# Mixture-of-experts stage: 71 slots of 256 rows become 60 slots of 256 rows and 15 tiles of 128 rows

## The reference

```
h = layernorm(x) * (1 + cb) + sb
logits = h @ router_w.T                      # 8 experts
weights, indices = top_k(softmax(logits), 2) # 2 of 8 for each of 8,192 tokens
weights = weights / (weights.sum(-1) + 1e-6)
gate, up = split(h @ w13[e])                 # 256 -> 2 x 512
y_e = (silu(gate) * up) @ w2[e]              # 512 -> 256
x = x + gb * sum over the two chosen e of weights * y_e
```

## Time and profile before

| | before |
|---|---|
| median of 3 runs | 1293.57 us (1293.27 to 1296.74) |
| time of the profiled execution | 1293.22 us |
| its span | 1291.4 us |
| expert stage, first to last matmul | about 713 to 1276 us |
| PE busy over the span | 1152.0 us, 89% |
| DVE / ACT / POOL busy | 906.8 / 713.2 / 929.5 us |

### The profile page before, as it was taken

The page is one execution under the profiler, slowest core; times in us unless marked ns, Lnnn a source line. Parts: engine busy times, 40 slices in busy tenths (PEclk is TensorE's granted clock), DMA queues, the critical chain, the costliest instruction groups (busy, mean ns, idle before and its releaser), DMA issues. The chain is left out here.

```text
span 1291.4 us, 53384 instructions
## 1 busy us (share of the span) xinstructions
PE 1152.0 (89%) x19576; PEld 978.8 (76%) x19576; DVE 906.8 (70%) x2387; ACT 713.2 (55%) x1419; POOL 929.5 (72%) x990
## 2 busy tenths in 40 slices
PE   4699999999999999999623899999999999999995
PEld 1477778888777777787413788888888888888884
DVE  2589999999999999999888544444444444444442
ACT  2378888988889888898533233333333333333331
POOL 3168999999899999999822466666666667676653
PEclk8599999999899999999655999999999999999998
DMA  8323343334333334333355688878788887888860
GB/s 223 82 69 82 94 138 116 90 106 123 100 104 111 106 108 118 97 118 101 100 155 148 124 137 128 136 136 134 137 135 137 127 131 136 133 139 136 136 108 1
DMA packets 201704, 153.07 MB, mean 119 GB/s; under 512 B 101658, under 2 KB 179570, under 8 KB 201330
## 3 DMA queue, kind: packets, MB, share of 16 engines
q0 software_dynamic: 32592, 56.75, 27.4%
q1 hardware_dynamic: 160770, 81.89, 25.0%
q10 hardware_dynamic: 8096, 11.01, 3.3%
HBM read 63.58 MB, written 44.04 MB: 83 GB/s over the span
## 5 line engine op out<-in xcount | busy, mean ns | idle before, releaser
L1298 PE MATMUL psum<-xT,xall 128*128 128x256 f16 x3408 | 384.8, 273 | 14.9 <-DMA xT<-grow 14.9
L1298 PEld LDWEIGHTS psum<-xT,xall 128*128 x3408 | 334.0, 98 | 54.3 <-issue 15.2
L1360 POOL DMA_INDIRECT out<-late,sidx x142 | 227.0, 1599 | 167.0 <-DVE late L1349 80.1
L1306 ACT ACTIVATE sg<-psum 128x512 f32<-128x512 f32 x142 | 84.8, 597 | 281.6 <-PE psum L1298 281.6
L1311 DVE SCALAR_TENSOR_TENSOR late<-psum,sg 128x512 f32<-128x512 f32 x142 | 98.2, 692 | 185.0 <-ACT sg L1306 182.9
L1278 POOL DMA_INDIRECT grow<-moe_rows,gidx x142 | 146.1, 1029 | 86.9 <-DVE gidx L1150 44.0
L1332 PE MATMUL psum<-w2s,hT 128*128 x1704 | 197.7, 273 | 2.8 <-DVE w2s L1386 2.6
L1332 PEld LDWEIGHTS psum<-w2s,hT 128*128 128x128 f16 x1704 | 166.6, 98 | 22.8 <-issue 3.4
L1322 DVE TENSOR_TENSOR hT<-late,hT 128x512 f16<-128x512 f32 x142 | 98.4, 693 | 98.7 <-ACT hT L1318 98.7
L1318 ACT ACTIVATE hT<-late 128x512 f16<-128x512 f32 x142 | 89.4, 629 | 112.0 <-DVE late L1311 112.0
L672 POOL TENSOR_TENSOR pT<-sc,pT 128x1024 f16<-128x1024 f32 x64 | 136.5, 2134 | 11.7 <-ACT pT L668 11.7
(11 more groups left out here) (262 smaller groups left out, 2294.2 us busy)
## 6 DMA issues: line engine op xcount, KB each, us to landing
stk<-qk SPq DMA_DIRECT2D x384, 64.0 KB, 2.9
moe_rows<-hrows SPq DMA_DIRECT2D x64, 256.0 KB, 3.6
out<-xall SPq DMA_DIRECT2D x64, 128.0 KB, 3.3
raw<-in_w ACTq DMA_DIRECT2D x26, 256.0 KB, 3.3
xall<-in_x ACTq DMA_DIRECT2D x16, 256.0 KB, 4.0
raw<-in_w SPq DMA_DIRECT2D x8, 512.0 KB, 8.9
xall<-in_x SPq DMA_DIRECT2D x8, 384.0 KB, 8.1
grow<-moe_rows,gidx POOLq DMA_INDIRECT x142, 4.7
```

The source lines that it names most:

```text
L1298: i = k.e.matmul(bank[:, n * LONG:(n + 1) * LONG], w13s[:, bass.ds(ex_reg * (G * 4 * I) + ((2 * c + b_) * 2 * I + col), P)], xT[:, k.x, a, ...
L1306: done(k.e.activation(sg[:, half, :], bGate[half][:, :], ACT.Silu, scale=1.0 / W_SCALE), "sg")
L1360: k.e.indirect_dma_start(out_rows, bass.IndirectOffsetOnAxis(ap=sidx[:, n:n + 1], axis=0), yo[:, k.v, q, :], None, bounds_check=B * T - 1, ...
```

## The change

The list has `NSLOT_TILES` = 135 tiles in place of 142: each expert's rows are now rounded up to whole tiles (128 + 7). Whole pairs of an expert's tiles are numbered first, then the odd ones. `NPAIRED` = 60 slots take tiles 0 to 119 in pairs as before; 15 slots, the singles, take the tiles 120 to 134 one by one. The units run in groups of five, `ORDER` = "PPSPP", 15 groups. With the counts given above there are 64 pairs and 3 odd tiles: tiles 120 to 127 are full tiles, 128 to 130 hold 111, 22 and 82 rows, and 131 to 134 hold none.

A pair unit is handled as a slot was. A single goes another way:

- `gate_up_by_token`: 12 matmuls in which the tile's transposed rows stand still and 512 columns of the weights move, into two PSUM banks of its own (6 and 7). The result has tokens on partitions.
- `silu_by_token`, `h_mul_by_token`, `h_hi_by_token`, `h_lo_by_token`: the same four steps, once for the tile, on 128 x 512.
- `h_trans`: two transposing DMAs on SP turn the high and the low part, since `down` needs hidden units on partitions. They are issued behind `x_trans` of the unit three places later.
- `down`: 12 matmuls of 256 columns. `gather`, `x_trans` and `scatter`: one transfer each.

Routing gets more DVE steps: pair and odd counts, three small maps that say where an expert's tiles lie, two steps on the tile numbers, and the expert of each slot in two passes. The router weights' ring `wrow` is `NWR` = 4 deep and its chain uses another semaphore.

```diff
-NSLOTS = (B * T * 2) // LONG + E - 1
-NSLOT_TILES = 2 * NSLOTS
+NSLOT_TILES = (B * T * 2) // P + E - 1
+NPAIRED = ((B * T * 2) // P - E) // 2
+NSLOTS = NSLOT_TILES - NPAIRED
+ORDER = "PPSPP"
...
+    def gate_up_by_token(k):
+        x_here(k)
+        k.product_done(1)
+        ex_reg = k.expert()
+        for c in range(G):
+            for a, b_ in PARTS:
+                for bank, at in ((bGate1, 0), (bUp1, I)):
+                    i = k.e.matmul(bank[:, :], xT[:, k.x, a, c, 0:P],
+                                   w13s[:, bass.ds(ex_reg * (G * 4 * I) + ((2 * c + b_) * 2 * I + at), I)],
...
+    def h_trans(k):
+        if k.n > 0:
+            k.e.wait_ge(S["y"], k.u - len(ORDER) + 1)
+        k.high_done()
+        k.e.dma_start_transpose(hT1[:, 0, :, :], hrow1[:, 0, :]).then_inc(s_hT, 16)
+        k.low_done()
+        k.e.dma_start_transpose(hT1[:, 1, :, :], hrow1[:, 1, :]).then_inc(s_hT, 16)
...
     def scatter(k):
         k.wait("yw")
-        k.wait_added(1)
-        for q in range(2):
-            n = 2 * k.t + q
+        k.moved(s_sc, V, k.u - 1)
+        for q, n in enumerate(k.tiles):
             k.e.indirect_dma_start(out_rows, ...
...
         @block.sync
         def _(e):
             route_sync(e)
-            for t in range(NSLOTS):
-                x_trans(Slot(e, t))
+            for u in range(NUNITS + NXT + 1):
+                k, single = unit(e, u), unit(e, u - NXT - 1)
+                if single and single.single:
+                    h_trans(single)
+                if k:
+                    x_trans(k)
...
+            for group in range(NUNITS // len(ORDER)):
+                gate_up(p0, 0)
+                gate_up(p0, 1)
+                if before:
+                    down(before)
+                gate_up(p1, 0)
+                gate_up(p1, 1)
+                down(p0)
+                gate_up_by_token(single)
+                down(p1)
+                gate_up(p2, 0)
+                gate_up(p2, 1)
+                gate_up(p3, 0)
+                down(single)
+                gate_up(p3, 1)
+                down(p2)
+            down(p3)
```

More of the change, by code:

```diff
@@ L1129, in route_vector @@
             if k == 0:
[L1130 to L1134, removed]
@@ L1150, in route_vector @@
         e.tensor_scalar(gidx[:, :], rowf[:, :], 0.0, None, ALU.max).then_inc(s_idx, 1)
[L1151 to L1154, removed]
+        for x_ in range(0, E - 1):
+            link(e.scalar_tensor_tensor(out=ex_of[:, :], in0=at, scalar=single_end[:, x_:x_ + 1],
                                         in1=ex_of[:, :], op0=ALU.is_ge, op1=ALU.add))
@@ L1267, in done @@
+            return expert_of[self.slot]
+    UNIT_OF_PAIR = [u for u in range(NUNITS) if not Unit(None, u).single]
     def done(ins, stage):
@@ L1337, in row_weights @@
     def row_weights(k):
[L1338 to L1343, removed]
+        k.moved(s_g, U, k.u)
+        late.link(k.e, k.e.tensor_tensor(gwm[:, k.r, 0:k.nq, :], grow[:, k.j, 0:k.nq, 2 * D:ROW],
+                                         bc_mid(oh_tile[:, k.slot, :], k.nq), ALU.mult))
+        k.wait("yw", NWR)
+        late.link(k.e, k.e.tensor_reduce(wrow[:, k.r, 0:k.nq], gwm[:, k.r, 0:k.nq, :], axis=X, op=ALU.add))
     def weigh(k):
         k.wait("y")
[L1346 to L1350, removed]
+        k.moved(s_sc, V, k.u - V)
+        for q in range(k.nq):
+            i = k.e.scalar_tensor_tensor(out=yo[:, k.v, q, :], in0=bY[k.y][:, q * D:(q + 1) * D],
+                                         scalar=wrow[:, k.r, q:q + 1], in1=grow[:, k.j, q, D:2 * D], op0=ALU.mult,
                                          op1=ALU.mult)
@@ L1371, in _ @@
             route_tensor(e)
-            for t in range(NSLOTS + 2):
-                now, late = slot(e, t - 1), slot(e, t - 2)
-                if now:
-                    gate_up(now, 0)
-                if now:
-                    gate_up(now, 1)
-                if late:
-                    down(late)
+            for group in range(NUNITS // len(ORDER)):
+                before, (p0, p1, single, p2, p3) = unit(e, group * len(ORDER) - 1), [unit(e, group * len(ORDER) + i) for i in range(5)]
+                gate_up(p0, 0)
[14 more added lines that the diff above has]
+            down(p3)
         @block.vector
@@ L1407, in _ @@
             route_scalar(e)
-            for t in range(NSLOTS):
-                for half in range(2):
-                    silu(Slot(e, t), half)
-                    h_hi(Slot(e, t), half)
+            for u in range(NUNITS):
+                k = unit(e, u)
+                if k.single:
+                    silu_by_token(k)
+                    h_hi_by_token(k)
+                else:
+                    for half in range(2):
+                        silu(k, half)
+                        h_hi(k, half)
         @block.gpsimd
@@ L1414, in _ @@
             route_gpsimd(e)
-            for t in range(NSLOTS + U - 1):
-                ahead, late = slot(e, t), slot(e, t - U + 1)
+            for u in range(NUNITS + U - 1):
+                ahead, late = unit(e, u), unit(e, u - U + 1)
                 if ahead:
```

253 lines of the change are left out of this document (177 added, 76 removed).

## The result

| | before, measured alongside | after |
|---|---|---|
| median | 1291.52 us (1287.61 to 1299.72, 20 runs) | 1285.53 us (1281.15 to 1294.59, 20 runs) |
| ratio, 95% interval | | 0.9968, 0.9953 to 0.9983 |
| profiled execution: its span | 1291.4 us | 1283.7 us |
| first to last matmul of the expert stage | 562.8 us | 555.6 us |

What follows compares the result with a forecast made beforehand. PE bounds the kernel, with the scatter chain right behind, taking over after the change: 1291.4 - 27.9 + 2.4 + 2.4 = 1268.3, + 15.1 for the chain = 1283.4 us, as a median 1285.5; range 1270 to 1298.

Steps and rivals of the forecast that it cites:

- PE's saving: PE in the expert stage: matmul time falls from 557.7 to 529.8 us, saving 27.9 us; a group takes 35.34.
- Routing: Routing on DVE and ACT: extra steps make `gidx` later and add 2.4 us to the path, bounds 0 and 3.5.
- The tail: Last scatters: the last two units become full pairs, landings cost at least 3.2 us each instead of 2.00, +2.4 us.
- There are 2.2 us to spare: SP's transposes before `down(single)`: ready at 8.3 us, due at 10.48, so free while POOL is less than 2.2 us late.
- The way that it named: With POOL over 2.2 us late, SP is held at a gather and PE waits at `down(single)`, 1 to 2 us a group.
- This is the term that decides: POOL's serial scatter chain: a group needs 36.68 us against PE's 35.34, so it ends 15.1 us behind PE.
- the single's link: Scatter chain: a single's scatter takes 5.80 us, a pair's 7.72 less one issue of 1.92; named as the likeliest error.
- The pair's link: Scatter chain: a pair's scatter stays at 7.65 to 7.80 us, taken as 7.72, from the trace before the change.
- Rival 1: PE stays the bound and the scatter chain keeps up, links averaging under 7.45 us: 1270 us, up to 1275; chance 0.2.
- Rival 2: More transposes lengthen scatter landings, making it slower: 1309 us at full, 1293 to 1298 partly; chance of over 1297.5: 0.12.
- The chip's clock: PE's clock: should not follow if PE waits a few us at `down(single)`, but left open; a fall would show as 0.50.
- the waits' lines: Sign in POOL's waits: nearly all of `out` for the DMA, few for DVE, if the scatter chain sets the pace.

Runs made afterwards that it cites:

- the second profile: The changed kernel, unaltered, measured and profiled once more against the kernel before: 1279.42 us, ratio 0.9923, expert stage 547.4 us.
- the run with both edits: Changed kernel with the single's transposes issued ahead of `x_trans(s+3)` and the expert's number loaded before the waits of `gate_up`: 1265.74 us, ratio 0.9800.
- the first experiment: Changed kernel with the expert's number read into PE's register before the waits of `gate_up` instead of behind them: 1280.57 us, ratio 0.9909.

## Why the number was right and the mechanism wrong

**PE's saving: right.** 27.9 us was worked out, from 35.34 us for a group. Where PE doesn't wait, a group takes just that: in the run with the transposes moved, from the end of one `gate_up_by_token` at 910.46 to the next at 945.80. The matmuls of 512 columns, bounded from the earlier trace rows, take 0.216 us: from 765.11 to the next matmuls at 767.70 it is 2.59 us for 12 (the 2.75 of the line run to the modelled end of the last).

```profile
765.11 2.75 PE L1382 MATMUL psum<-xall,xT 128*128 x12
```

**Routing: right.** +2.4 us was forecast. From the first step of routing on DVE to the last step of `gidx` it was 29.80 us and is 32.12, +2.3; the first matmul starts 1.9 us later behind the same point. The attention half before it, which the change leaves alone, ended 2.9 us sooner in this execution (between 661 and 669 us in the profiles), so 2.9 of the 7.7 us between the two spans are not the change's.

**The tail: mis-sized.** +2.4 was forecast, +0.5 measured. The last landing is waited for 2.97 us in place of 2.00, near the 3.2 taken; but it is the only one that counts, since the scatter before it waits for DVE (2.72 us) and not for a landing.

**"There are 2.2 us to spare": the step that failed first.** Two of its numbers were short. The rows of s+3 were there later than +1.2: at +3.9 in the timeline above, whose last gather started at -0.7 (-3.2 to -2.6 at 11 other singles), and the transposes left the queue at +6.8 to +9.2, not +6.3. And the transposes landed not 2 us behind their issue but, at the eight stalls in the two profiles of the changed kernel, 3.6 to 6.6 us. The prediction had its bound at a gather's 4.7 and took 2, between the ends, without a row for it. With 4.5 in place of 2 the spare is -0.3 us even if POOL is on time. There is a slip in the sum too: a gather issued at -2.5 lands by its 4.7 us at +2.2, not +1.2, which alone takes 1.0 of the 2.2 us. The way that it named, SP held at a gather and PE waiting at `down(single)`, is what happened; but its condition, POOL more than 2.2 us late, was not needed. It held at the single of the timeline, whose gather was 2.5 us late; at the other stalls of that profile, and at all ten of the run without the singles' scatters, POOL was on time.

**"This is the term that decides": the step that fell.** The scatter chain was to end 15.1 us behind PE. Three things speak against it: with 15 links fewer the stage stayed at 555.6 us; with all links kept but the transposes issued first it fell to 538.7; and in that run the chain's links average 35.0 us a group, just under PE's 35.34. The size that was wrong is above all the single's link: 5.80 was taken, the pair's less one issue, and it is 5.0 in the mean there and 4.8 in the middle. With 5.0 and the pair's 7.72 left as it was, a group is 35.88 us and the lag 0.5 us, not 1.34; with the pair's 7.5 there is none. The prediction had named this itself as where it would be wrong above all. The pair's link was taken from a stretch of the trace of before whose pace need not be the chain's floor; its last link ends at a wait for DVE. That a term of 15.1 us was wrong and the time right is chance: PE stood still by another way. Its idle time in the stage, over the matmuls worked out, was 562.8 - 557.7 = 5.1 us before and 555.6 - 529.8 = 25.8 after, 20.7 us more, nearly all at the two places named. So the stage has -27.9 + 20.7 = -7.2 us; with routing's +1.9, the tail's +0.5 and the -2.9 of the attention half that makes the -7.7 us of the spans. And 14.2 of the 20.7 us are of a sort that the second profile doesn't have (last section), so even this way to 1285.5 us belongs in part to one execution.

**The rivals.** Rival 1, "PE stays the bound", 1270 us, was wrong for the kernel as changed and right in that the chain doesn't bind: with the transposes moved ahead that is the time, 1269.34 us. Rival 2, landings of the scatters lengthened by more transposes, is not seen: in the run with the transposes moved, which has all 30 of them, a pair's link averages 7.5 us, under the 7.65 to 7.80 of before. But the transposes themselves land late. The rule of the Trainium skill ("DMA: Bandwidth & Descriptors", "Queues, rings and completion order"), that a semaphore increment lands only behind the earlier writes of its DMA engine, would make a transpose's landing wait for scatters and gathers in flight; 3.6 to 6.6 us agree with that, but no run here takes away the transfers that are in flight at that time, so it is not shown.

**The chip's clock.** Left open was whether it would fall when PE waits a few us. It did not: 1.00 over the stretch in which PE stands still 17 us.

## What to carry to other kernels

Give a transfer its place on an in-order queue by when its data are ready, and never behind an instruction that waits for a later unit's data: moving two issues one unit forward took the ratio from 0.9968 (0.9923 in the second measurement) to 0.9828, more than the whole change had gained. A stall taken away in front of one that binds later only moves (1.2 us less before `gate_up(p3)`, 1.3 more before `down(single)`, both stages 538.7 us), so look at the length of the stage and not at the stall's line; and a spare of 2 us that rests on a landing nobody has measured is no spare. When a forecast time comes out, still look whether its releasers are those forecast: here the waits' lines gave the first doubt. They are no proof: the run with the transposes moved has 26 waits for landings, 60.5 us in all, that cost PE nothing. What decides is to take the suspected work away and read the stage.

## What the hardware showed that was not expected

**Landings of small transposes.** A transposing DMA of 128 x 512 fp16 from on-chip memory mostly takes SP 1.2 to 1.3 us to issue, and where PE waited for it, its rows were usable 3.6 to 6.6 us behind the end of the issue in the two profiles of the changed kernel, and 1.4 to 7.4 us in all profiles with these transposes, with gathers and scatters in flight. Where PE did not wait, the landing isn't seen; in places it must have been under 2.7 us. Two of the longest, 7.4 us, are why `down(single)` still waits in the run with both edits.

**Late signals in one execution.** In the profile of the changed kernel ACT starts on some products 0.7 to 1.7 us later than PE ends them allows, over 20 times, 23 us in all. In the timeline below the first 24 of 48 matmuls end near 1142.6, ACT begins at 1144.02 with PE as its releaser (elsewhere it is 2.8 us behind the start of the matmuls, here 4.09), DVE's product ends at 1145.40, and the next `gate_up` begins at 1146.40 instead of 1145.2:

```profile
1139.93 5.40 PE L1350 MATMUL psum<-xT,xall 128*128 128x256 f16 x48
...
1144.02 0.60 ACT L1358 ACTIVATE sg<-psum 128x512 f32<-128x512 f32 x1 [4.47 <-PE psum L1350]
1144.71 0.69 DVE L1363 SCALAR_TENSOR_TENSOR late<-psum,sg 128x512 f32<-128x512 f32 x1 [3.36 <-issue]
...
1146.40 2.81 PE L1350 MATMUL psum<-xT,xall 128*128 128x256 f16 x24 [1.07 <-issue]
```

None of the other nine profiles has such a signal, that of the same kernel run again among them. All 12 stalls at `gate_up(p3)` of the first profile stand behind such a signal, which fits the 14.2 us there and the 1.7 us in the other; why the signals were late stays open. The changed kernel doesn't bring them each time, and a study that had looked at this one profile alone would have taken them for a cost of the change, as the first experiment did.
